# Indirect transfers in groups of eight, and the first mixture's routing moved out of the memory attention

## The reference, cut to what matters

```python
x = x + _L0_attn_ref(_layernorm(x), ...)               # a0
x = x + _L0_xattn_ref(ctx_1024, _layernorm(x))         # w0, time warping
x = x + _L0_ffn_ref(_layernorm(x), ...)                # f0, three fast-feedforward trees q, k, v, then an attention of them
x = x + _L1_attn_ref(...)                              # a1
x = x + _L1_xattn_ref(_layernorm(x), ctx_1024, ...)    # x1, memory attention
x = x + _L1_ffn_ref(_layernorm(x), ...)                # f1, mixture: a shared expert and 8 experts, top 2
...                                                    # a2, x2, f2, a3, x3
x = x + _L3_ffn_ref(_layernorm(x), ...)                # f3, mixture with a capacity for each expert
```

```python
for _ in range(DEPTH):
    score = jnp.einsum('nd,nd->n', xf, node_w[cur]) + node_b[cur]
    cur = 2 * cur + 1 + (score >= 0).astype(jnp.int32)
hidden = relu(einsum('nd,ldh->lnh', xf, w1) + b1[:, None, :]) * one_hot(leaf).T[:, :, None]
out = einsum('lnh,lho->no', hidden, w2) + one_hot(leaf) @ b2
```

```python
expert_values, expert_indices = jax.lax.top_k(softmax(x @ gate_w + gate_b), k=2)
weights_E = (one_hot(expert_indices) * expert_values[..., None] / sum).sum(axis=2)
return x + _mlp(x, shared) + einsum('bse,bsed->bsd', weights_E, all_outputs)
```

## Time and profile before

| | us |
|---|---|
| runs of the kernel | 2447.25 median (2441.56, 2447.25, 2456.69) |
| profiled execution | 2444.76 |
| its span | 2443.0 |
| trees f0 | 396.9 to 793.4 |
| memory attention x1 | 975.5 to 1115.9 |
| first mixture f1 | 1115.9 to 1402.0 |
| last mixture f3 | 2148.5 to 2443.0 |

### The profile page before, as it was taken

How to read it: one execution, slowest core, us unless ns; L and a number is a source line. 1 busy time by engine, 2 the same in 40 slices (tenths; PEclk the granted TensorE clock), 3 DMA queues, 4 the chain that set the end, 5 groups by cost and what they waited for, 6 DMA issues and landing times. The chain is left out here.

```text
span 2443.0 us, 39516 instructions
## 1 busy us (share of the span) xinstructions
PE 1783.7 (73%) x14484; PEld 1216.3 (50%) x14484; DVE 1336.7 (55%) x3646; ACT 1101.9 (45%) x2273; POOL 746.8 (31%) x718
## 2 busy tenths in 40 slices
PE   4886635549867798676699578687878868842995
PEld 2554524215434466454489555355545545542774
DVE  3887597302212576555233446686439969963233
ACT  3774522113332576763144234576347747710331
POOL 1233101540252332225335300332123322156353
PEclk9988876769987799887799879799979979965997
DMA  4111460213530500201257500100000010011224
GB/s 157 82 82 82 129 209 22 60 58 99 160 106 15 220 17 3 64 32 36 81 162 234 186 0 1 35 33 14 1 3 2 2 35 28 10 41 54 67 77 139
DMA packets 145171, 173.18 MB, mean 71 GB/s; under 512 B 21074, under 2 KB 120594, under 8 KB 144050
## 3 DMA queue, kind: packets, MB, share of 16 engines
q1 hardware_dynamic: 125252, 129.09, 16.7%
q0 software_dynamic: 13248, 28.21, 3.4%
q10 hardware_dynamic: 6480, 13.37, 1.5%
HBM read 126.84 MB, written 79.05 MB: 84 GB/s over the span
## 5 line engine op out<-in xcount | busy, mean ns | idle before, releaser
L1151 PE MATMUL a_AV<-a_vx,a_pT 128*64 128x18 f32 (+1 forms) x3072 | 114.0, 223 | 32.7 <-DVE a_two L821 14.8
L1013 ACT ACTIVATE a_e<-a_e 128x512 f32<-128x512 f32 x192 | 110.2, 622 | 60.5 <-DVE a_e L843 60.4
L1151 PEld LDWEIGHTS a_AV<-a_vx,a_pT 128*64 128x64 f32 x3072 | 104.9, 145 | 61.9 <-issue 27.8
L2055 PE MATMUL f_Y<-f_h,f0w 128*128 128x512 f32 x128 | 79.0, 702 | 71.7 <-ACT f_h L1936 61.1
L1138 PE MATMUL a_TP<-ident,a_e 128*128 128x128 f32 x768 | 108.7, 286 | 19.5 <-ACT a_e L1013 18.9
L1018 ACT COPY a_pT<-a_TP 128x512 f32<-128x512 f32 x192 | 103.5, 588 | 41.2 <-PE a_TP L1138 41.1
L843 DVE TENSOR_TENSOR a_e<-a_S,a_mx 128x1024 f32<-128x1024 f32 x96 | 117.3, 1221 | 2.9
L1138 PEld LDWEIGHTS a_TP<-ident,a_e 128*128 128x128 f32 x768 | 89.3, 146 | 57.9 <-ACT a_e L1013 47.8
L1127 PE MATMUL a_S<-a_kbd,a_qT 64*64 64x512 f32 x768 | 115.5, 677 | 1.0 <-issue 0.6
L1936 ACT ACTIVATE f_h<-f_H,f_b 128x512 f32<-128x512 f32 x64 | 44.0, 687 | 151.8 <-PE f_H L2046 81.0
L3606 POOL DMA_INDIRECT f_back<-f_ys,f_row x78 | 74.7, 957 | 115.2 <-DVE f_ys L3695 103.3
(11 more groups left out here) (544 smaller groups left out, 4685.3 us busy)
## 6 DMA issues: line engine op xcount, KB each, us to landing
f_wt<-in_f_ew SPq DMA_DIRECT2D x39, 584.0 KB
f_slots<-in_blank SPq DMA_DIRECT2D x1, 18576.0 KB
f_wt<-in_f_leaf SPq DMA_DIRECT2D x94, 98.0 KB
f_xs<-f_slots SPq DMA_DIRECT2D x47, 144.0 KB
memory_x_k<-w_stage ACTq DMA_DIRECT2D x24, 256.0 KB, 3.1
f_slots<-in_blank SPq DMA_DIRECT2D x1, 5760.0 KB
f_xs<-leaf_slots SPq DMA_DIRECT2D x22, 256.0 KB
leaf_out<-f_ys SPq DMA_DIRECT2D x22, 256.0 KB
```

Of the source, the lines that this page charges most:

```text
L1013: act.activation(eh, eh, ACT.Exp).then_inc(weights.sem, 1)
L1151: last = pe.matmul(AV[64 * c:64 * c + 64, 2 * hp * W1:2 * (hp + 1) * W1], pT[:, hp, 64 * c:64 * c + 64], vx[:, g % 2, t, c, 2 * hp:2 * hp ...
L2055: ins = pe.matmul(Y[:, :], w2[:, c, :], h[:, m % 2, :], start=False, stop=c == NC - 1)
```

## The change

Four edits.

In the trees, POOL waits after every eighth scatter until all so far have landed, and so between k and v; before the gathers of v it waits for the last gathers of k, and among them after every eight. The second line of work begins three steps later.

```diff
-    ROWS_FROM = 23
-    LAST = NM - ROWS_FROM + 5
+    ROWS_FROM = 26
+    LAST = 46
...
                 for t in range(NT):
+                    if t and t % 8 == 0:
+                        pool.wait_ge(scattered[r].sem, scattered[r].after(t - 1))
+                    elif r and t == 0:
+                        pool.wait_ge(scattered[0].sem, scattered[0].after(NT - 1))
                     pool.indirect_dma_start(out=slots[r][:, :], out_offset=bass.IndirectOffsetOnAxis(ap=slot[:, r, t:t + 1], axis=0),
                                             in_=xn[:, t, :], in_offset=None).then_inc(scattered[r].sem, 16)
...
+            for u in range(2):
+                pool.wait_ge(k_in[u].sem, k_in[u].after(NG // 2 - 1))
             for g in range(NG):
+                if g and g % 2 == 0:
+                    pool.wait_ge(v_in[g - 2].sem, 16 * GT)
+                    pool.wait_ge(v_in[g - 1].sem, 16 * GT)
                 for t in range(GT):
```

```diff
-def memory_attention(nc, k, d, tag, r):
+def memory_attention(nc, k, d, tag):
...
-            r.load(sp)
-            WR = d["f1_sh"].shape[1]
-            sp.dma_start(k.f0w[:, NB * SL:NB * SL + WR], d["f1_sh"]).then_inc(k.shared_in, 16)
...
-                if g - 4 in (0, 2):
-                    r.root(pool, (g - 4) // 2)
-            r.scatter(pool, 0)
...
-                if i - 3 in batch:
-                    r.make_shares(v, batch[i - 3], no_fill)
-                    r.pick(v, batch[i - 3], no_fill)
-                    r.weigh(v, batch[i - 3])
...
-        phases[5] = lambda: mixture(nc, k, d, "f1", shared=True, r=routers["f1"])
+        phases[5] = lambda: routed(nc, k, d, "f1", shared=True)
...
-        phases[11] = lambda: routed(nc, k, d, "f3", shared=False, store=out)
+        phases[11] = lambda: routed_small(nc, k, d, "f3", shared=False, store=out)
```

The first mixture is now made by `routed` with four batches of eight tiles, all in its own stage. It waits before each run of eight but the first (`c` is the token's first or second expert):

```diff
-    BT, NBAT = 4, NT // 4
+    BT, NBAT = 8, NT // 8
...
                 for c in range(2):
+                    if b or c:
+                        pool.wait_ge(scattered.sem, scattered.after(BT * (2 * b + c) - 1))
                     for t in range(BT * b, BT * b + BT):
                         pool.indirect_dma_start(out=slots[:, :], out_offset=bass.IndirectOffsetOnAxis(ap=slot[:, c, t:t + 1], axis=0),
                                                 in_=pay[:, c, t, :], in_offset=None).then_inc(scattered.sem, 16)
-                if b + 3 < NBAT:
-                    root(b + 3)
+                if b == 0:
+                    root(3)
```

The last mixture is made by `routed_small`, the old `routed` with batches of four and one wait a batch:

```diff
+                pool.wait_ge(copied.sem, copied.after(b))
+                if b:
+                    pool.wait_ge(scattered.sem, scattered.after(2 * BT * b - 1))
+                for c in range(2):
```

More of the change, by code:

```diff
@@ L2493, in _ @@
                     score(i)
-                if i - 2 in batch:
-                    pe.wait_ge(r.xT_ready.sem, r.xT_ready.after(batch[i - 2]))
                 if within(i - 1):
@@ L2499, in _ @@
                     turn(i + 1)
-                if i - 4 in batch:
-                    r.place(pe, batch[i - 4])
                 if within(i - 1):
@@ L2938, in routed @@
     CAP = max(8, int(max(1, NB * SL * 2 // E) * 1.25))
+    BT, NBAT = 8, NT // 8
+    BLK = 256
+    NBLK = 2 * NB * SL // BLK + E - 1
+    RX, RY, RWT, RR = (8 if shared else 4), 3, 4, 6
+    if shared:
+        groups = [(None, None, 2) for _ in range(NBLK)]
+    else:
+        groups = [(e, lo, min(4, CAP // P - lo)) for e in range(E) for lo in range(0, CAP // P, 4)]
+    NGR = len(groups)
+    GW = max(n for _, _, n in groups)
+    slots, back = k.slots[tag], k.back[tag]
+    WR = d["f1_ew"].shape[1]
@@ new lines, in routed @@
+    sent = [ph.counter(f"sent{r}", 16) for r in range(RY)]
+    back_in, x_added, stored = [ph.counter(f"back_in{b}", 16) for b in range(NBAT)], ph.counter("x_added"), ph.counter("stored", 16)
+    if shared:
+        counted, table_ready = ph.counter("counted"), ph.counter("table_ready")
+        sh_hidden, sh_ready, sh_out, sh_taken = ph.counter("sh_hidden", F), ph.counter("sh_ready", F), ph.counter("sh_out"), ph.counter("sh_taken")
+        wt_in = [ph.counter(f"wt_in{r}", 16) for r in range(RWT)]
@@ new lines, in routed, with sent_after, weights @@
+    sent_by = [sum(n for j, (_, _, n) in enumerate(groups) if j % RY == r) for r in range(RY)]
+    NSH = NB * SL // 512 if shared else 0
+    n_early = 16 * 4
+    n_late = 16 * (5 if shared else 4)
+    W = BT * E
+    def sent_after(i):
+        return 16 * sum(n for j, (_, _, n) in enumerate(groups) if j % RY == i % RY and j <= i)
+    def weights(i):
+        if not shared:
+            e = groups[i][0]
+            return w1[:, e, :], w2[:, e, :, :], b1[:, F * e:F * e + F], b2r[:, e, :]
+        return parts(wt[:, i % RWT, :])
@@ L2939, in routed, with routed_small @@
+    ph.close()
+def routed_small(nc, k, d, tag, shared, store=None):
+    ph = Phase(nc, tag)
+    E, F = 8, 4
+    CAP = max(8, int(max(1, NB * SL * 2 // E) * 1.25))
     BT, NBAT = 4, NT // 4
```

1082 lines of the change are left out of this document (452 added, 630 removed).

## The result

| | before | after |
|---|---|---|
| median of the runs, us | 2444.4 (2441.11 to 2456.69, 4 runs) | 2378.22 (2371.75 to 2381.66, 4 runs) |
| profiled execution, us | 2444.76 | 2371.75 |
| its span, us | 2443.0 | 2370.0 |

The ratio is 0.9717, with a 95% interval of 0.9676 to 0.9758: 66 us faster. The forecast was 2365, in a range of 2335 to 2402.

What follows compares the result with a forecast made beforehand. Releases arriving late while POOL issues indirect transfers without a pause were taken as the bound. Trees -69, memory attention -24, first mixture +10, last +1 give -82, so 2362.8 profiled and a median of 2365, range 2335 to 2402.

Steps and rivals of the forecast that it cites:

- What bounds: Trees, scatters and gathers of v: releases arriving late while POOL issues indirect transfers without a pause, not any engine's work.
- Trees, scatters: Trees, 64 scatters: waits after each eight keep relus going, so step 26 comes at 519.7 instead of 560.0, -40 us.
- Trees, end: Trees, leaf steps to end: gathers of v begin at 670.3, end at 724 against 793.4, -69 us for the trees.
- The rule: Trees: by the skill's port rule PE and ACT lose nothing to POOL's issuing, so pauses could give nothing back; forecast rejected it.
- Memory attention: All routing leaves this stage: seven update intervals of 11.12 us, plus 3 us for loads and last scatters, -24 us.
- First mixture: It takes over the whole routing: first turn of sorted rows 124.7 us after its start instead of 114.7, +10 us (+3 to +25).
- I add 3 for late hand-overs: First mixture: shared products end about when POOL's run does, at 121.7 us, so 3 us more cover late hand-overs.
- my slower rival: First mixture: each run of eight scatters delays a hand-over by 8.85 us, +50; trees not cured; 2490 us, chance 4%.
- Last mixture: Last mixture's scatters: seven waits add 9, powers inside waits -5, less late hand-overs -3, +1 us (-4 to +8).
- The sum: Whole kernel: -69 - 24 + 10 + 1 = -82 us, so 2362.8 for the profiled execution and a median of 2365.
- The pauses cure nothing: Rival, trees: releases are late from the number of transfers or a reason outside POOL; about 0 gain, 2448 us, chance 6%.
- Half a cure: Rival, trees: each run of eight costs what k's gathers did (5.34 us), trees only -35, total 2403 us, chance 15%.

Runs made afterwards that it cites:

- late set: Nothing changed in the kernel: a set of runs in which the kernel before took 2438 to 2444 us and its stalls beside indirect transfers appear.
- on time: Nothing changed in the kernel: sets of runs in which the kernel before took 2301 and 2295 us; the stalls are gone from their traces.
- the even pitch: Kernel before with a 128x256 memset before every scatter and gather of v in the trees, and waits after every four router scatters: 2343.51 us, ratio 0.9600.

## Why the prediction was right, and where it was not

**What bounds.** Right for a late set: releases come late while POOL issues without a pause. The trace of one execution could not show that this is a condition which comes and goes. That the result was measured in a late set is luck: on time the same forecast is wrong by its sign.

**Trees, scatters** (-40 forecast, step 26 at 519.7). The relu of step 26 comes at 502.66 in the changed kernel. I had misread the steps: counted from the first, the relus at 460.12 and 560.03 are those of steps 8 and 24, not 6 and 23, so 4.5 us of my way to step 26 were two steps too many. The 12 us of loss that I kept for the relus did not come before the leaf steps either: from step 8 to step 26 it takes 45.5 us here and on time. A loss came right behind: from step 26 to the gathers of v it took 166.8 us (502.7 to 669.5) instead of the 149 I carried over, since leaf steps and the last three runs of eight now lie side by side (9.38 and 6.00 idle above). On time it is 148.2. These are two errors of 17 us with opposite signs, so it is luck that the gathers began at 669.5 where I had 670.3.

**Trees, end** (-69). Measured -69.6 with the closing barrier: 32 gathers from 669.47, and the last update of x ends at 723.9, forecast 724. (I had set 724 against 793.4, which holds the barrier; against the last update before, 792.2, it is -68. And 18.62 and 38 are 56.6, not 55.) The sum was right, by the luck just named, and the mechanism in so far as breaks in the issuing cure it; that they need to be breaks was wrong.

**The rule.** The Trainium skill (SBUF — State Buffer, "Who interferes with whom") says that only the port pair shared by DVE and GpSimd causes contention. The traces agree with it as far as it goes: on time PE is busy 59.00 of 59 us beside the same issuing. In late sets PE is busy 10.93 of 59 beside it, so a rule on ports is no promise that hand-overs are on time.

**Memory attention** (-24): the mechanism was right, the size off. The mis-sized term is seven intervals of 11.12, 77.8 us; measured 69.1, since the last two are 7.94 and 3.49. Drawn out of the earlier trace rows, where the last interval (10.7) held the router's work, I took a steady pace for a pipeline that drains. The rest (3 us forecast) measured 1.2.

**First mixture** (+10, up to +25): measured +27.7. The first scatter came 25.8 us in (forecast 26), the sorted rows were loaded from 122.9 on (forecast 118), nearly right. The term that failed is "I add 3 for late hand-overs": the shared products, which I had put at about the same end as POOL's run, ended at 139.8 (on time at 122.3). In a chain of hand-overs PE to DVE to ACT beside scatters in eights, DVE idled for 14.44 and 11.48 us and ACT for 14.19 and 7.16 where on time the same waits take 7.29, 7.05, 7.02 and 4.79. On time the first turn comes at 126.7, so late releases are 13 of the 15 us that my sum lacks up to the turn; another 2.7 are behind it. This is the mechanism of my slower rival at a smaller price: the stage is 27.7 us longer, where the rival has 50. Scatters here start 1.49 us apart on the mean (1039.77 to 1133.84), and still releases are late; the rate that is harmless to the relus is not harmless to this part. Why, no run tells.

**Last mixture** (+1): +2.0, within what traces of this stage differ by. Five of the waits come behind a power and cost 1.0 us of idle time each, two come without one and cost 2.1.

**The sum** (-82, to 2362.8 for the profiled execution). Measured 2371.75. The memory attention gave 7 us more than forecast, the first mixture took 18 more, the last 1 more, the trees came out as forecast, and stages that I had left unchanged gave 2. The median of the runs stands 6.5 us above the profiled one instead of 2.5; so 2378 where I had 2365.

**The rivals.** "The pauses cure nothing": its time (2448) is about what the change without waits gave in a late set (2443). It is refuted for late sets; on time there is nothing to cure, and the change is slower by 1.7%. I gave 0.04 to slower; on time it was so in all runs. The evidence on the page could not have told me; a spread of the times by sets could have. "Half a cure" (2403, trees -35) fell by the trees' -69.6. My range up to 2402 took in about half of that case, not most of it as I wrote.

## What to carry to other kernels

Spacing indirect transfers costs little and can save much: 0.2 us more between two of them gave 76 to 83 us back in the late condition (396 and 403 to 320 in the trees). On time waits after every eight cost 9 to 13 us; the even pitch was not run there. Spacing needs no wait for the landing; a short operation of the same engine does, if it is longer than the gap that the engine leaves anyway. Compare a kernel only with one timed beside it, and stage by stage: here the same kernel differed by 6% from set to set. And work put ahead into another stage has to be priced at both ends: the router in the memory attention cost 31 us there and saved 28 in late sets while its scatters came unspaced, but with spaced scatters 27 to 31 against 41 to 48, and on time 24 against 46.

## What I had not expected of the hardware

- The same program with the same transfers, each as fast, took 2301 or 2440 us by the set of runs, and what the traces show of the difference lies nearly all in the stages with runs of indirect transfers. In one set PE was busy 59.00 of 59 us beside 47 scatters, in another 10.93 beside 46.
- A small change of pace decides: a transfer every 1.28 us was too fast in the late condition, one every 1.44 to 1.48 us was not, for the relus (nothing between was run); for a chain of many short hand-overs 1.49 in runs of eight still was.
- Late semaphore updates queue up: four of PE's came 3.7, 11.6, 21.7 and 38.0 us after its work, and a late trace holds 149 to 153 of the scatters' 1024 updates where one on time holds 1013 or more.
- A memset of 0.12 us before each transfer left the pitch at 1.27 us (0.96 busy, 0.12, the rest idle); one of 0.33 us made it 1.46.
- A wait for the landing of eight scatters cost 1.53 to 2.13 us of idle time in place of 0.30.
